# An LSTM step on one core: the low half of h in group 1 made in two operations, each with a wait of its own

## The chip, the cores and the metric

The kernel runs on 1 core of one Trainium2 chip. The metric is the device time of one execution in microseconds (us). TensorE multiplies matrices, VectorE (DVE in the rows), ScalarE (ACT) and GpSimd (POOL) work element by element, and SyncE (SP) issues transfers. The engines run side by side and wait for each other on semaphores. PE and PEld in the rows are TensorE's matmuls and its loads of the stationary operand.

## The reference

An LSTM over 512 steps, batch 16, 512 features, with a residual; one weight matrix for the input and one for h, all in fp32:

```python
xW = jnp.einsum('ntd,dg->ntg', x, Wx) + b
def step(carry, xw_t):
    prev_h, prev_c = carry
    a = xw_t + prev_h @ Wh
    i, f, o = (jax.nn.sigmoid(a[:, k * 512:(k + 1) * 512]) for k in range(3))
    g = jnp.tanh(a[:, 3 * 512:])
    next_c = f * prev_c + i * g
    next_h = o * jnp.tanh(next_c)
    return (next_h, next_c), next_h
x = x + jnp.swapaxes(hs, 0, 1)
```

(The gates are written shorter here than in the original; `hs` are the h of all steps.)

## The kernel before

**Numbers.** Each fp32 operand is split into an fp16 high part and an fp16 low part (what the high part leaves), so that a product is high times high, low times high and high times low. The weights are split once at the start. x is split in chunks of 16 steps, and h in every step. `h_halves[par]` holds for each of the 4 blocks of features (128 features each, 16 columns of batch) three slots of 16 columns: zeros, the high half, the low half. Slots 0 and 1 together are the stationary operand of `recurrent_low` (times the low weights), slots 1 and 2 that of `recurrent_high` (times the high weights).

**Groups.** The features of h come in two groups, `n` = 0 with blocks 0 and 1 and `n` = 1 with blocks 2 and 3. The gates' sums of a group lie in `acc[par][:, n]`, and each sum needs all four blocks of the h of the step before. A block takes four matmuls, one for each quarter of 32 rows of the array.

**TensorE in a step** (from L356): low weights with blocks 0 and 1 for both groups, when the high half of group 0 is there; high weights with blocks 0 and 1 for group 0, when the low half of group 0 is there; low weights with blocks 2 and 3 for group 0; then L363 waits for the low half of group 1, high weights with blocks 2 and 3 for group 0, and `acc_ready` goes up for the first time. The rest of group 1 follows, and `acc_ready` goes up again. Then come matmuls for the input of a later pair of steps (`input_part`, L303). L311 is the matmul of `recurrent_low`, L317 that of `recurrent_high`.

**VectorE in a step**, written out in order by hand: transpose group 0's sums when `acc_ready` allows it (`turn(0)`, L510), add the two halves (L514), transpose group 1's (L510), products of the gates (L523), L514 and new cell (L528) and so on. The end of the step, which the change touches, is: high half of h of group 0 (L538), new cell of group 1 (L528), `full_h(0)` (L542), `keep_cell(0)` (L532), `low_of_h(0)` (L547), `high_of_h(1)` (L538), `full_h(1)` (L542), `keep_cell(1)` (L532), `low_of_h(1)` (L547), and the output of the step (L575). L547 waits for L542. L538 waits for ScalarE's tanh of the cell (L270) and GpSimd's output gate (L194). L575 waits for the kept cell, L532.

**Behind the output** stands some work of preparing x, set by the place `at` of the step in its chunk: in steps 1 to 4 a quarter of the next chunk is searched for its largest value (L586), in 5 to 10 there are one or two operations of one to four columns (L590, L433, L436, L439, L443, L447, L450), in 12 to 15 the low half of a quarter of x is made (`low_of_x`, L493), and in 0 and 11 there is nothing. Chunk 0 also makes the last two quarters of its own x in its steps 1 and 2. The last chunk prepares nothing. Then the next step's `turn(0)` comes.

ScalarE does the tanh of the gates (L260, L265) and of the cell, opens the sums (L234, L237) and makes the high half of x (L216). GpSimd adds the output gate of group 0 (L186) and scales it (L194).

Of the kernel before, what the change touches and what calls it, by code (L numbers as in the profile page):

```python
# [5 lines left out]
ALU = mybir.AluOpType  # L6
# [9 lines left out]
NG = 2  # L16
# [7 lines left out]
def lstm_kernel(nc, x, h0, wx, wh, bias, out):  # L24
# [7 lines left out]
    with ExitStack() as ctx:  # L32
# [6 lines left out]
        def sem(name):  # L39
            return ctx.enter_context(nc.semaphore(name))  # L40
# [85 lines left out]
        acc_ready = sem("acc_ready")  # L126
# [10 lines left out]
        h_feat_ready = sem("h_feat_ready")  # L137
        h_ready = sem("h_ready")
# [150 lines left out]
        @block.tensor  # L289
        def _(pe):  # L290
            pe.wait_ge(ones_ready, 2)
            pe.wait_ge(tops_ready, 1)
            pe.matmul(wx_sums[:, 0:1], ones[:], tops[:, 0:1], start=True, stop=True).then_inc(sums_ready, 1)
            pe.wait_ge(x_top_ready, 1)
            pe.matmul(x_sums, ones_16[:], x_top[:], start=True, stop=True).then_inc(x_sum_ready, 1)
            pe.wait_ge(tops_ready, 2)
            pe.matmul(wh_sums[:, 1:3], ones[:], tops[:, 1:3], start=True, stop=True).then_inc(sums_ready, 1)

            def input_part(pair, of):
                for c in of:  # L300
                    for half, w in ((0, w_high["wx"]), (1, w_high["wx"]), (0, w_low["wx"])):
                        for j in range(Q):
                            last = pe.matmul(x_acc[pair % 2][32 * j:32 * j + 32], x_halves[:, pair % (CHUNK // 2), c, half],  # L303
                                             w[:, c].rearrange("p (n q) g -> p q n g", q=Q)[:, j],
                                             start=False, stop=False, skip_group_check=True)
                return last

            def recurrent_low(par, n, of):
                for c in of:
                    for j in range(Q):  # L310
                        pe.matmul(acc[par][32 * j:32 * j + 32, n, 0:GL], h_halves[1 - par][:, c, 0:2], w_low["wh"][:, c, n * Q + j],  # L311
                                  start=False, stop=False, skip_group_check=True)

            def recurrent_high(par, n, of):
                for c in of:
                    for j in range(Q):
                        last = pe.matmul(acc[par][32 * j:32 * j + 32, n, 0:GL], h_halves[1 - par][:, c, 1:3], w_high["wh"][:, c, n * Q + j],  # L317
                                         start=False, stop=c == C - 1, skip_group_check=True)
                return last

            pe.wait_ge(wx_low_done, C)
            pe.wait_ge(zeroed, 6)
            for p in range(2):
                for n in range(NG):
                    for j in range(Q):
                        opened = pe.matmul(acc[p][32 * j:32 * j + 32, n, 0:GL], h_halves[0][:, 0, 0:2], w_high["wx"][:, 0, j],
                                           start=True, stop=False, skip_group_check=True)
                    opened.then_inc(acc_opened, 1)
            for i in range(2):
                for j in range(Q):  # L330
                    opened = pe.matmul(x_acc[i][32 * j:32 * j + 32], h_halves[0][:, 0, 0:2],
                                       w_high["wx"][:, 0].rearrange("p (n q) g -> p q n g", q=Q)[:, j],
                                       start=True, stop=False, skip_group_check=True)
                opened.then_inc(acc_opened, 1)
            pe.wait_ge(x_ready, 1)
            pe.wait_ge(bias_placed, 1)
            input_part(0, (0, 1, 2, 3)).then_inc(x_summed, 1)
            pe.wait_ge(bias_placed, 2)
            input_part(1, (0, 1))
            pe.wait_ge(acc_filled, 1)  # L340
            pe.wait_ge(h_ready, NG)
            for c in range(C):
                pe.wait_ge(wh_low_done, c + 1)
                recurrent_low(0, 0, (c,))
                first = recurrent_high(0, 0, (c,))
                recurrent_low(0, 1, (c,))
                second = recurrent_high(0, 1, (c,))
                if c == C - 1:
                    first.then_inc(acc_ready, 1)
                    second.then_inc(acc_ready, 1)  # L350

            for t in range(T):
                par = t % 2
                chunk, at = divmod(t, CHUNK)
                if t > 0:
                    pe.wait_ge(h_high_ready, NG * t + 1)  # L356
                    recurrent_low(par, 0, (0, 1))
                    recurrent_low(par, 1, (0, 1))
                    pe.wait_ge(h_ready, NG * t + 1)
                    recurrent_high(par, 0, (0, 1))  # L360
                    pe.wait_ge(h_high_ready, NG * t + 2)
                    recurrent_low(par, 0, (2, 3))
                    pe.wait_ge(h_ready, NG * t + 2)  # L363
                    recurrent_high(par, 0, (2, 3)).then_inc(acc_ready, 1)
                    recurrent_high(par, 1, (0, 1))
                    recurrent_low(par, 1, (2, 3))
                    recurrent_high(par, 1, (2, 3)).then_inc(acc_ready, 1)
                if at == 6 and chunk + 1 < CHUNKS:
                    pe.wait_ge(x_top_ready, chunk + 2)
                    pe.matmul(x_sums, ones_16[:], x_top[:], start=True, stop=True).then_inc(x_sum_ready, 1)  # L370
                if t + 1 < T:
                    pair = (t + 3) // 2
                    if 2 * pair >= T:
                        pe.wait_ge(acc_filled, t + 2)
                    elif t % 2 == 1:
                        if at == 13:
                            pe.wait_ge(x_ready, QUARTERS * (chunk + 1) + 1)
                        pe.wait_ge(bias_placed, pair + 1)
                        input_part(pair, (0,))
                        pe.wait_ge(acc_filled, t + 2)  # L380
                        input_part(pair, (1,))
                    else:
                        input_part(pair, (2,))
                        pe.wait_ge(acc_filled, t + 2)
                        input_part(pair, (3,)).then_inc(x_summed, 1)

        @block.vector
        def _(dve):
# [60 lines left out]
            def inverses_of(par):  # L449
# [32 lines left out]
            dve.tensor_scalar(h_halves[1][:, :, 1, :], h0_feat[:], scales[0][:, 2:3], None, ALU.mult).then_inc(h_high_ready, NG)  # L482
            dve.wait_ge(h_high_ready, NG)
            dve.scalar_tensor_tensor(h_halves[1][:, :, 2, :], h0_feat[:], scales[0][:, 2:3], h_halves[1][:, :, 1, :],
                                     ALU.mult, ALU.subtract).then_inc(h_ready, NG)
            dve.wait_ge(b_loaded, 16)
            dve.tensor_scalar(b_rows[:, :, 64:GL], b_rows[:, :, 64:GL], 0.5, None, ALU.mult).then_inc(b_ready, 1)

# [12 lines left out]
            for t in range(T):  # L501
                par = t % 2
# [3 lines left out]
                nth = [NG * t + n + 1 for n in range(NG)]  # L506
# [24 lines left out]
                def keep_cell(n):  # L531
                    dve.scalar_tensor_tensor(gates[1 - par][n][:, 0, :], products[n][:, 0, :], 0.5, products[n][:, 1, :],  # L532
                                             ALU.mult, ALU.add).then_inc(cell_kept, 1)

                def high_of_h(n):
                    og, ct = (k.rearrange("p (c b) -> p c b", b=B) for k in (o_gate[n][:], cell_tanh[n]))
                    dve.wait_ge(h_parts_ready[n], 2 * (t + 1))
                    dve.tensor_tensor(h_halves[par][:, 2 * n:2 * n + 2, 1, :], og, ct, ALU.mult).then_inc(h_high_ready, 1)  # L538
# [2 lines left out]
                    og, ct = (k.rearrange("p (c b) -> p c b", b=B) for k in (o_gate[n][:], cell_tanh[n]))  # L541
                    dve.tensor_tensor(h_feat[par][:, 2 * n:2 * n + 2, :], og, ct, ALU.mult).then_inc(h_feat_ready, 1)  # L542

                def low_of_h(n):
                    cs = slice(2 * n, 2 * n + 2)
                    dve.wait_ge(h_feat_ready, nth[n])
                    dve.tensor_tensor(h_halves[par][:, cs, 2, :], h_feat[par][:, cs, :], h_halves[par][:, cs, 1, :], ALU.subtract)\  # L547
                        .then_inc(h_ready, 1)

# [11 lines left out]
                new_cell(1)  # L561
                full_h(0)
                keep_cell(0)
                low_of_h(0)
                high_of_h(1)
                full_h(1)
                keep_cell(1)
                low_of_h(1)
                dve.wait_ge(cell_kept, NG * (t + 1))

                half, slot = divmod(at, HALF)
# [76 lines left out]
```

## Time and profile before

| | |
|---|---|
| median of 3 runs | 1855.11 us (1855.08 to 1855.83) |
| the profiled execution, its own time | 1856.47 us |
| its span in the profile | 1854.4 us |
| busy: VectorE, TensorE matmuls, TensorE loads, ScalarE, GpSimd | 92%, 90%, 57%, 55%, 29% |
| instructions of VectorE | 9739 |

The span is that of the instructions in the trace; the device time includes some 2 us around it. Busy time adds the recorded durations. On VectorE and TensorE one instruction often begins before the recorded end of the one in front, so a gap smaller than that overlap shows as no idle time; starts are read from the rows in order of time.

### The profile page before, as it was taken

The page shows a single profiled execution, that of the slowest core. Times are in us where ns is not written, and L with a number is a line of the kernel's source. Part 1 is how long each engine was busy: PE and PEld are TensorE (multiplying, and loading weights), DVE is VectorE, ACT ScalarE, POOL GpSimd, SP SyncE. Part 2 cuts the span into 40 slices and gives each one's busy share as a digit, 9 for nine tenths or more (in the row PEclk, how much of TensorE's full clock was granted, in tenths as well). Part 3 has the DMA queues.
Part 4 walks back from the last instruction along what each step waited for, and adds up shares of the span by engine and source line. Part 5 has one row for each costly group of instructions (what it writes and reads, how often), then busy time and mean ns, then how long its engine had stood idle before and what let it go on. Part 6 is the DMA issues. An engine that isn't in the chain of part 4 may idle for free.

```text
span 1854.4 us, 106048 instructions
## 1 busy us (share of the span) xinstructions
PE 1674.3 (90%) x45116; PEld 1065.3 (57%) x45116; DVE 1713.2 (92%) x9739; ACT 1011.4 (55%) x3985; POOL 539.3 (29%) x1560
## 2 busy tenths in 40 slices
PE   1999999999999999999999999999999999999997
PEld 0555555555555555555555555555555555555555
DVE  8999999999999999999999999999999999999998
ACT  4555555555555555555555555555555555555554
POOL 0222223322332222233223332222232233322222
PEclk9999999999999999999999999999999999999999
DMA  5000000000000000000000000000000000000000
GB/s 210 15 26 21 21 23 23 21 21 26 21 21 26 21 21 21 26 21 21 26 21 21 26 21 21 21 27 21 21 26 21 21 24 24 21 21 27 18 12 14
DMA packets 39067, 49.03 MB, mean 26 GB/s; under 512 B 4416, under 2 KB 36160, under 8 KB 38592
## 3 DMA queue, kind: packets, MB, share of 16 engines
q1 hardware_dynamic: 37152, 37.77, 6.3%
q8 instruction: 352, 5.77, 1.3%
q10 hardware_dynamic: 1440, 4.49, 0.6%
q14 instruction: 123, 1.01, 0.2%
HBM read 25.46 MB, written 16.78 MB: 23 GB/s over the span
## 4 chain that ended last, share of the span: by engine, by line
DVE 70%; PE 19%; ACT 7%; issue 3%; DMA 1%; ACTq 0%; DVEq 0%
DVE turned L510 22%; DVE mailbox L514 13%; PE acc L311 12%; DVE products L523 11%; ACT gates L260 7%; PE acc L317 7%; DVE h_halves L538 5%; DVE h_halves L547 3%; DVE gates L532 3%; DVE x_halves L493 3%; DVE out_ring L575 3%; DVE h_feat L542 3%; DVE x_tops L586 2%; DVE mailbox L528 2%; DMA wh<-in_wh 1%
## 5 line engine op out<-in xcount | busy, mean ns | idle before, releaser
L311 PE MATMUL acc<-wh_low,h_halves 128*32 128x256 f16 x16384 | 719.4, 274 | 135.6 <-DVE h_halves L538 133.8
L317 PE MATMUL acc<-wh_high,h_halves 128*32 128x256 f16 x16384 | 722.3, 275 | 0.0
L303 PE MATMUL x_acc<-wx_high,x_halves 128*32 128x512 f16 x8192 | 621.5, 380 | 1.1 <-ACT x_acc L234 1.1
L311 PEld LDWEIGHTS acc<-wh_low,h_halves 128*32 128x32 f16 x16384 | 390.5, 96 | 395.3 <-DVE h_halves L538 383.8
L260 ACT ACTIVATE gates<-mailbox 128x96 f32<-128x96 f32 x1024 | 257.1, 251 | 634.1 <-DVE mailbox L514 634.1
L510 DVE STREAM_TRANSPOSE turned<-acc 128x256 f32<-128x256 f32 x1024 | 458.9, 448 | 57.2 <-PE acc L317 51.4
L194 POOL TENSOR_SCALAR o_gate<-gates,scales 128x32 f32<-128x32 f32 x1024 | 372.7, 364 | 419.4 <-ACT gates L265 419.4
L186 POOL TENSOR_TENSOR o_preact<-turned 128x32 f32<-128x32 f32 x512 | 163.4, 319 | 892.0 <-DVE turned L510 892.0
L317 PEld LDWEIGHTS acc<-wh_high,h_halves 128*32 128x32 f16 x16384 | 343.6, 96 | 113.8
L303 PE MATMUL x_acc<-wx_low,x_halves 128*32 128x512 f16 x4096 | 399.2, 380 | 0.0
L237 ACT ACTIVATE acc<-x_acc,step_mask 128x512 f32<-128x512 f32 x512 | 334.8, 654 | 4.7 <-PE x_acc L303 4.7
L514 DVE TENSOR_TENSOR mailbox<-turned 128x96 f32<-128x96 f32 x1024 | 270.2, 264 | 17.6
L303 PEld LDWEIGHTS x_acc<-wx_high,x_halves 128*32 128x32 f16 x8192 | 216.7, 97 | 117.3 <-issue 3.7
L523 DVE SCALAR_TENSOR_TENSOR products<-gates 128x64 f32<-128x64 f32 x1024 | 230.4, 225 | 55.3
L270 ACT ACTIVATE mailbox<-mailbox 128x32 f32<-128x32 f32 x1024 | 191.5, 187 | 163.7 <-DVE mailbox L528 163.7
L265 ACT ACTIVATE gates<-o_preact 128x32 f32<-128x32 f32 x1024 | 231.9, 226 | 0.0
L528 DVE SCALAR_TENSOR_TENSOR mailbox<-products 128x32 f32<-128x32 f32 x1024 | 200.9, 196 | 0.0
L547 DVE TENSOR_TENSOR h_halves<-h_feat,h_halves 128x32 f16<-128x32 f32 x1024 | 196.6, 192 | 0.0
L538 DVE TENSOR_TENSOR h_halves<-o_gate,mailbox 128x32 f16<-128x32 f32 x1024 | 189.5, 185 | 0.0
L532 DVE SCALAR_TENSOR_TENSOR gates<-products 128x32 f32<-128x32 f32 x1024 | 189.5, 185 | 0.0
L542 DVE TENSOR_TENSOR h_feat<-o_gate,mailbox 128x32 f32<-128x32 f32 x1024 | 184.1, 180 | 0.0
L303 PEld LDWEIGHTS x_acc<-wx_low,x_halves 128*32 128x32 f16 x4096 | 109.9, 97 | 112.0 <-issue 1.0
(67 smaller groups left out, 696.5 us busy)
## 6 DMA issues: line engine op xcount, KB each, us to landing
out<-out_ring SPq DMA_DIRECT2D x128, 128.0 KB, 2.1
x_ring<-in_x SPq DMA_DIRECT2D x120, 128.0 KB, 2.9
wx<-in_wx ACTq DMA_DIRECT2D x4, 512.0 KB, 8.1
wx<-in_wx SPq DMA_DIRECT2D x4, 512.0 KB, 8.1
wh<-in_wh SPq DMA_DIRECT2D x4, 512.0 KB, 16.7
wh<-in_wh ACTq DMA_DIRECT2D x4, 512.0 KB, 17.1
x_ring<-in_x SPq DMA_DIRECT2D x2, 512.0 KB, 16.7
b_rows<-in_b ACTq DMA_DIRECT2D x1, 256.0 KB, 21.4
```

The source lines that it names most:

```text
L194: pool.tensor_scalar(o_gate[n][:], gates[par][n][:, 4, :], 1.0, scales[following][:, 1:2], ALU.add, ALU.mult)\
L237: act.activation(acc[t % 2][:, :, 0:GL], x_acc[t // 2 % 2][:], ACT.Copy, scale=step_mask[:, t % 2:t % 2 + 1])\
L260: act.activation(gates[par][n][:, 1:4, :], preact[n].rearrange("p (g c) b -> p g (c b)", c=2), ACT.Tanh, scale=rescale[chunk % 2]).then_in ...
L303: last = pe.matmul(x_acc[pair % 2][32 * j:32 * j + 32], x_halves[:, pair % (CHUNK // 2), c, half], w[:, c].rearrange("p (n q) g -> p q n g ...
L311: pe.matmul(acc[par][32 * j:32 * j + 32, n, 0:GL], h_halves[1 - par][:, c, 0:2], w_low["wh"][:, c, n * Q + j], start=False, stop=False, sk ...
L317: last = pe.matmul(acc[par][32 * j:32 * j + 32, n, 0:GL], h_halves[1 - par][:, c, 1:3], w_high["wh"][:, c, n * Q + j], start=False, stop=c ...
L510: dve.transpose(turned[n][:].rearrange("p g s b -> p (g s b)"), acc[par][:, n, 0:GL]).then_inc(turned_ready, 1)
L514: dve.tensor_tensor(preact[n], turned[n][:, 0:6, 0, :], turned[n][:, 0:6, 1, :], ALU.add)\
L523: dve.scalar_tensor_tensor(products[n][:], gates[par][n][:, 2:4, :], 1.0, gates[par][n][:, 0:2, :], ALU.add, ALU.mult).then_inc(products_r ...
L532: dve.scalar_tensor_tensor(gates[1 - par][n][:, 0, :], products[n][:, 0, :], 0.5, products[n][:, 1, :], ALU.mult, ALU.add).then_inc(cell_k ...
L538: dve.tensor_tensor(h_halves[par][:, 2 * n:2 * n + 2, 1, :], og, ct, ALU.mult).then_inc(h_high_ready, 1)
L547: dve.tensor_tensor(h_halves[par][:, cs, 2, :], h_feat[par][:, cs, :], h_halves[par][:, cs, 1, :], ALU.subtract)\
```

## The change

`low_of_h` took a group and made the low half of both of its blocks in one operation. It now takes the first block, the number of blocks and the number of the `full_h` of this step that it waits for. Group 0 is made in one operation as before. Group 1 is made in two operations in a row, block 2 and block 3, each of which counts up `h_ready`. TensorE waits for the first ahead of the high weights with block 2, and for the second ahead of those with block 3. `h_ready` goes up three times a step instead of two, and its waits are counted so.

```diff
-            pe.wait_ge(h_ready, NG)
+            pe.wait_ge(h_ready, 3)
...
-                    pe.wait_ge(h_ready, NG * t + 1)
+                    pe.wait_ge(h_ready, 3 * t + 1)
                     recurrent_high(par, 0, (0, 1))
                     pe.wait_ge(h_high_ready, NG * t + 2)
                     recurrent_low(par, 0, (2, 3))
-                    pe.wait_ge(h_ready, NG * t + 2)
-                    recurrent_high(par, 0, (2, 3)).then_inc(acc_ready, 1)
+                    pe.wait_ge(h_ready, 3 * t + 2)
+                    recurrent_high(par, 0, (2,))
+                    pe.wait_ge(h_ready, 3 * t + 3)
+                    recurrent_high(par, 0, (3,)).then_inc(acc_ready, 1)
...
-                                     ALU.mult, ALU.subtract).then_inc(h_ready, NG)
+                                     ALU.mult, ALU.subtract).then_inc(h_ready, 3)
...
-                def low_of_h(n):
-                    cs = slice(2 * n, 2 * n + 2)
-                    dve.wait_ge(h_feat_ready, nth[n])
+                def low_of_h(first, blocks, kept):
+                    cs = slice(first, first + blocks)
+                    dve.wait_ge(h_feat_ready, NG * t + kept)
...
-                low_of_h(0)
+                low_of_h(0, 2, 1)
                 high_of_h(1)
                 full_h(1)
                 keep_cell(1)
-                low_of_h(1)
+                low_of_h(2, 1, 2)
+                low_of_h(3, 1, 2)
                 dve.wait_ge(cell_kept, NG * (t + 1))
```

## Rows read from the trace of the kernel before

**Rows 1.** The page: busy time, the clock by slices, the chain that ended last

```profile
PE 1674.3 (90%) x45116; PEld 1065.3 (57%) x45116; DVE 1713.2 (92%) x9739; ACT 1011.4 (55%) x3985; POOL 539.3 (29%) x1560
...
PEclk9999999999999999999999999999999999999999
...
DVE 70%; PE 19%; ACT 7%; issue 3%; DMA 1%; ACTq 0%; DVEq 0%
```

**Rows 2.** The waits: who waited for whom, us in total, times, longest

```profile
PE acc L311 <- DVE h_halves L538: 133.8, 480, 1.7
DVE turned L510 <- PE acc L317: 51.4, 201, 0.4
```

**Rows 3.** Timeline of VectorE (start us, us, ...): first and last opening transpose

```profile
51.18 0.45 DVE L510 STREAM_TRANSPOSE turned<-acc 128x256 f32<-128x256 f32 x1
...
1848.96 0.45 DVE L510 STREAM_TRANSPOSE turned<-acc 128x256 f32<-128x256 f32 x1 [0.38 <-PE acc L317]
```

**Rows 4.** Timeline of all engines, end of a step with nothing behind L575

```profile
1010.95 0.18 DVE L542 TENSOR_TENSOR h_feat<-o_gate,mailbox 128x32 f32<-128x32 f32 x1
...
1011.05 0.19 DVE L532 SCALAR_TENSOR_TENSOR gates<-products 128x32 f32<-128x32 f32 x1
...
1011.16 0.19 DVE L547 TENSOR_TENSOR h_halves<-h_feat,h_halves 128x32 f16<-128x32 f32 x1
1011.20 0.39 PE L311 MATMUL acc<-wh_low,h_halves 128*32 128x256 f16 x8
...
1011.27 0.28 DVE L575 SCALAR_TENSOR_TENSOR out_ring<-h_feat,inverses,x_ring 128x64 f32<-128x64 f32 x1
1011.41 0.34 PEld L317 LDWEIGHTS acc<-wh_high,h_halves 128*32 128x32 f16 x16
...
1011.86 0.45 DVE L510 STREAM_TRANSPOSE turned<-acc 128x256 f32<-128x256 f32 x1 [0.31 <-PE acc L317]
```

**Rows 5.** Timeline of VectorE: ends of steps with L493, and with L586

```profile
1007.75 0.28 DVE L575 SCALAR_TENSOR_TENSOR out_ring<-h_feat,inverses,x_ring 128x64 f32<-128x64 f32 x1
1007.95 0.48 DVE L493 SCALAR_TENSOR_TENSOR x_halves<-x_ring,scales,x_halves 128x256 f16<-128x256 f32 x1
1008.35 0.45 DVE L510 STREAM_TRANSPOSE turned<-acc 128x256 f32<-128x256 f32 x1
...
1014.79 0.28 DVE L575 SCALAR_TENSOR_TENSOR out_ring<-h_feat,inverses,x_ring 128x64 f32<-128x64 f32 x1
1014.99 0.41 DVE L586 TENSOR_REDUCE x_tops<-x_ring 128x1 f32<-128x256 f32 x1
1015.38 0.45 DVE L510 STREAM_TRANSPOSE turned<-acc 128x256 f32<-128x256 f32 x1
```

**Rows 6.** Timeline of VectorE in chunk 0: L493 and L586 in one step

```profile
57.81 0.48 DVE L493 SCALAR_TENSOR_TENSOR x_halves<-x_ring,scales,x_halves 128x256 f16<-128x256 f32 x1
58.21 0.41 DVE L586 TENSOR_REDUCE x_tops<-x_ring 128x1 f32<-128x256 f32 x1
58.54 0.44 DVE L510 STREAM_TRANSPOSE turned<-acc 128x256 f32<-128x256 f32 x1
```

**Rows 7.** Groups of instructions: form xcount | busy us, mean ns | idle before

```profile
L547 DVE TENSOR_TENSOR h_halves<-h_feat,h_halves 128x32 f16<-128x32 f32 x1024 | 196.6, 192 | 0.0
...
L532 DVE SCALAR_TENSOR_TENSOR gates<-products 128x32 f32<-128x32 f32 x1024 | 189.5, 185 | 0.0
...
L443 DVE TENSOR_SCALAR acc_scale<-x_scale_bits,scale_bits,top_scale 128x1 f32<-128x1 f32 x32 | 8.6, 270 | 0.1
```

**Rows 8.** Timeline of VectorE before the steps: operations of one column in a row

```profile
33.81 0.14 DVE L466 COPY factors<-inverse_bits 128x1 f32<-128x1 f32 x1
33.87 0.14 DVE L467 TENSOR_SCALAR factors<-inverse_bits 128x1 f32<-128x1 f32 x1
```

**Rows 9.** L317 (1011.38 to 1011.6) and L311 (one step): ns min/median/max

```profile
L317 PE MATMUL acc<-wh_high,h_halves x8: 272/275/278, 1011.4 to 1011.5; 128*32 128x256 f16 x8
...
L311 PE MATMUL acc<-wh_low,h_halves x32: 272/273/283, 1010.5 to 1012.0; 128*32 128x256 f16 x32
```

## The prediction

> **What bounds the kernel now.** I read the page first. VectorE is busy 92% of the span, TensorE 90% at the full clock (the granted clock is 9 or more tenths in every slice, which is the 2.4 GHz level), and the chain that ended last runs 70% through VectorE and 19% through TensorE [rows 1]. So the kernel is one chain of 512 steps, and the waits say where it changes hands: TensorE waits for the high half of h (L538) in 480 cases, VectorE waits for TensorE's sum before the transpose (L510) in 201 cases, and nobody is listed as waiting for the low half (L547) [rows 2]. First and last opening transpose are 1797.78 us apart, 511 steps of 3.518 us on the mean [rows 3].
>
> Then I read one step in order of time, because a list of idle time hides ties. In a plain step (1011 us) the second L547 starts at 1011.16, L575 at 1011.27, and the next transpose only at 1011.86 after 0.31 us of idling for TensorE [rows 4]. So here TensorE sets the end: its loads of the stationary operand for `recurrent_high(par, 0, (2, 3))` start at 1011.41, and 0.45 us later the transpose starts. In a step that also makes the low half of x (L493), the order is L575 at 1007.75, L493 at 1007.95, transpose at 1008.35, and in one that searches x (L586) L575 at 1014.79, L586 at 1014.99, transpose at 1015.38 [rows 5]. All three kinds of step take the same 3.52 us from transpose to transpose (1008.35, 1011.86, 1015.38 [rows 4, 5]). The question is whether VectorE has slack in the last two. The first chunk tells: there L493 and L586 stand one behind the other, with no wait between them: L493 at 57.81, L586 at 58.21, transpose at 58.54, and TensorE is long done [rows 6]. L493 therefore holds VectorE for 0.40 us and L586 for 0.33 us by themselves. L575 plus L493 is 0.20 + 0.40 = 0.60 us from L575 to the transpose, against 0.59 us (1011.27 to 1011.86) that TensorE needs anyway. **In steps with L493 VectorE has no slack at all; with L586 it has 0.59 - 0.20 - 0.33 = 0.06 to 0.07 us; in all others at least 0.2 us** (the largest of the small operations behind L575 takes 0.27 us, L443 [rows 7], and VectorE operations free their engine about 0.08 us before their recorded end: L542 takes 0.18 and the next starts 0.10 behind it [rows 4]).
>
> **The change, part by part.**
> 1. VectorE: one 128x32 operation at the end of the step becomes two of 128x16, so 512 more operations. L547 takes 192 ns, L532 of the same width 185 ns [rows 7]. By width, L586 (256 columns, 0.41 us) against L532 (32) is 1.0 ns a column and L493 (256, 0.48 us) 1.3 ns [rows 5, 7]; so 16 columns less save 16 to 21 ns: I take 17, or 175 ns an operation (an estimate). What counts for the queue is start to start. L542 takes 0.18 us and the next operation starts 0.10 us behind it [rows 4]; I take the overlap as 83 ns, so that L547 holds VectorE for 192 - 83 = 109 ns, which agrees with the 0.11 us from L547 to L575. A piece: 175 - 83 = 92; I take 91 ns, so the two hold VectorE for 0.182 instead of 0.109 us: **+73 ns** for L575 and all behind it. Bounds: an operation of one element holds it about 62 ns (0.06 from 33.81 to 33.87 [rows 8]), +15 ns; a piece as dear as a whole operation, 109 ns, +109 ns. 91 is the value of the slope between these ends, the upper one being the nearer row (the same operation). The wait of the second piece on `h_feat_ready` is met already by the first, so it costs nothing.
> 2. TensorE: the wait is split. Block 2's low half ends at 1011.16 + 0.175 = 1011.335, 17 ns earlier than now, and with the 0.05 us from the end of L547 to the load (1011.35 to 1011.41 [rows 4]) its loads could start at 1011.39. But the matmuls before them (8 of L311 from 1011.20, two batches of four side by side at 0.11 us a batch) hold the array until 1011.41, so only the lateness of the load goes. That lateness is visible: the first matmuls behind this wait took 278 ns, the ordinary ones 272 to 273 [rows 9]. Gain: **-6 ns** at most on TensorE's path, bounds 0 and -6.
> 3. Block 3's low half starts one piece later, 1011.25, and ends at 1011.43; its loads can start at 1011.48. Its matmuls are due one batch behind those of block 2, at 1011.41 + 0.11 = 1011.52, and a load that comes just in time costs 10 ns (283 against 273 ns for L311 behind its wait [rows 9]). So it is ready with 0.03 us to spare and the second wait costs nothing. If that cover is gone (a piece over 0.12 us start to start), each ns comes onto every step. Queued behind it on TensorE are the last four matmuls of group 0, whose end the transpose waits for, and all of group 1.
> 4. The counts `3 * t + ...` of `h_ready`, the initial increment by 3, and the call for group 0 change no instruction.
>
> Where the stall goes: in a plain step TensorE is still last, 6 ns earlier. In a step with L493 the transpose starts 73 ns later, since VectorE had no slack. In one with L586, 73 less the slack of 66 is +7 ns. The chain from a transpose on is unchanged, the second transpose of a step follows its own predecessor (L514), so the late transposes move everything behind them.
>
> Sum over 511 intervals, taken from the profiled execution:
> - 31 chunks x 4 steps with L493 = 124, x 73 ns = +9.05 us
> - 124 steps with L586 x 7 ns = +0.87 us; two of them, in chunk 0, have L493 as well and pay 66 more: +0.13 us
> - the other 263 x -6 ns = -1.58 us
> In all **+8.5 us**. The profiled execution was 1856.47 us (span 1854.4), 1.36 above the median of the runs, 1855.11. On the median: 1855.11 + 8.5 = **1863.6 us**, +0.46%.
>
> The Trainium skill ("VectorE: DVE Perf Modes", the TRN2 errata) states a fixed cost for each SBUF operation, 58 cycles plus one per column at 0.96 GHz, and warns that many small tiles pay it each time. By that an operation of 32 columns is 94 ns (the 0.10 us between L542 and L532 agrees) and one of 16 is 77 ns; the shift would be +60 ns and the sum, an estimate with that page's figures, +5.2 us, so 1860.3.
>
> **The rivals.**
> - *Pieces nearly as dear as the whole* (as forecast, larger term). For it: L532 and L547 differ in what they write and read, not in width, by 7 ns, and by the slopes above the whole width of 32 is 32 to 42 of the 192 ns. At 109 ns a piece: 124 x 109 + 124 x 43 = +18.9 us, no gain on TensorE (block 3 becomes ready at 1011.51, just in time): 1874.0. Between this and the forecast all is possible; 1 in 10 for the upper half of it.
> - *Not slower: the added operation is hidden and only TensorE's gain is left.* Place: the interval L493 to transpose. If L493 frees VectorE 0.07 us sooner than its 0.40 us, the transposes wait for TensorE in all steps, and 511 x -6 ns = -3.1 us: 1852.0. It decides when the pair costs no more than the old one, that is under 0.055 us a piece, or when L493 has slack. For it: 0.395 is just what TensorE's time leaves, and such a tie looks like a wait for TensorE. Against it: the same 0.40 us stands at 57.81, where the next operation waits for nobody. 7 in 100.
> - *A piece waits until the one in front has ended*, the pieces in series at 0.175 us. L575 would start 0.158 us later: 124 x 158 = +19.6, 124 x 92 = +11.4 us; block 3 would be ready at 1011.56 and its matmuls at 1011.57 instead of 1011.52, some +49 ns in the other 263: +12.9. Sum +43.9 us: 1899.0. Against it: L532 starts well before the end of L542 [rows 4]. 3 in 100. The Trainium skill ("VectorE: DVE Perf Modes", "The DRAIN you can't avoid") says that the next operation does not start until the pipe is empty; the rows here show starts some 80 ns ahead of the recorded end, so the trace does not bear out that rule in this form.
> - *TensorE pays for the second wait.* Place: the load for block 3, which can no longer run a whole batch ahead. Its price is 10 ns where it is late: 263 x (10 + 6) = +4.2 us on the sum above, 1867.8. From 0.12 us a piece on. 8 in 100, inside my range.
>
> **How the numbers follow.** Forecast, the term between +50 and +95 ns: 72 in 100, 1859 to 1870. Dearer pieces 10, second wait 8, serial 3, hidden 7. No change that can be measured here is within 0.2%, 3.7 us (1851.4 to 1858.8). Hidden falls within it, with -0.17%, and so do very cheap pieces. Slower by more 0.88, same 0.09, faster 0.03. At +50 ns a step the sum is 6.2 - 0.7 - 1.6 = +3.9 us, 1859.0; the range goes to 1858 below, and above to 1873, near the sum of the bound of 109 ns.
>
> **What would show each step.** Two operations of 128x16 at about 175 ns, 90 ns apart; L575 0.18 instead of 0.11 us behind the first; steps with L493 at 3.59 us, those with L586 at 3.52, plain ones at 3.511; 0.20 + 0.40 us from L575 to transpose in the first; the first matmuls of block 2 at 273 instead of 278 ns; no idle time of TensorE in front of block 3. The prediction is wrong if steps with L493 keep 3.517 us, if plain steps lengthen, or if a piece takes over 0.2 us.

## The result: 1861.4 us, 0.33% slower

The changed kernel takes 1861.41 us (median of 7 runs, 1861.28 to 1861.64); the kernel before took 1855.23 us beside it (7 runs, 1855.08 to 1855.83). That is +6.2 us, a ratio of 1.0033 with a 95% interval of 1.0021 to 1.0045. The interval goes from +3.9 to +8.3 us. The forecast was 1863.6 us, +8.5, just above it.

The profiled execution after took 1861.64 us, its span is 1859.5 us. Page of the kernel after: busy time, then the chain that ended last by engine.

```profile
PE 1672.8 (90%) x45116; PEld 1071.7 (58%) x45116; DVE 1737.4 (93%) x10251; ACT 1012.0 (54%) x3985; POOL 540.4 (29%) x1560
...
DVE 71%; PE 17%; ACT 8%; issue 3%; DMA 1%; ACTq 0%; DVEq 0%
```

VectorE has 512 instructions and 24 us more; the chain has moved from TensorE to VectorE, as far as a share of 2 points shows it. The waits say the same: the transpose waits visibly for TensorE in 171 steps, where it was 201 [rows 2].

```profile
DVE turned L512 <- PE acc L317: 34.1, 171, 0.4
```

Groups by form after the change (mean ns behind the comma). `low_of_h` is now L549, the transpose L512, the output L578, the low half of x L495, the search of x L589.

```profile
L549 DVE TENSOR_TENSOR h_halves<-h_feat,h_halves 128x16 f16<-128x16 f32 x1024 | 133.8, 172 | 0.0
L549 DVE TENSOR_TENSOR h_halves<-h_feat,h_halves 128x32 f16<-128x32 f32 x512 | 98.2, 192 | 0.0
```

A piece takes 172 ns on the mean (175 was estimated), 175 the first and 169 the second: half the width saves 20 of 192 ns. Now the end of a step of each kind, in order of time. First a plain step (place 11), the counterpart of [rows 4].

```profile
996.56 0.26 DVE L549 TENSOR_TENSOR h_halves<-h_feat,h_halves 128x16 f16<-128x16 f32 x2
996.59 0.39 PE L311 MATMUL acc<-wh_low,h_halves 128*32 128x256 f16 x8
996.74 0.28 DVE L578 SCALAR_TENSOR_TENSOR out_ring<-h_feat,inverses,x_ring 128x64 f32<-128x64 f32 x1
996.79 0.35 PEld L317 LDWEIGHTS acc<-wh_high,h_halves 128*32 128x32 f16 x16
996.81 0.61 PE L317 MATMUL acc<-wh_high,h_halves 128*32 128x256 f16 x16
...
997.25 0.45 DVE L512 STREAM_TRANSPOSE turned<-acc 128x256 f32<-128x256 f32 x1 [0.23 <-PE acc L317]
```

The output starts 0.18 us behind the first piece, not 0.11. TensorE's loads start at 996.79, 0.02 us ahead of the matmuls. Before, in the step of [rows 4], loads and matmuls both read 1011.41:

```profile
1011.41 0.62 PE L317 MATMUL acc<-wh_high,h_halves 128*32 128x256 f16 x16
```

There is no idle time in front of the matmuls with block 3: by the starts in the two traces they come 109 ns behind those with block 2 on the mean over all steps, where it was 115 ns before. The first eight of these matmuls (four with block 2, four with block 3), by duration (min/median/max):

```profile
L317 PE MATMUL acc<-wh_high,h_halves x8: 272/273/273, 996.8 to 996.9; 128*32 128x256 f16 x8
```

The 278 ns of [rows 9] are gone. Then steps with L495 (1004.40 to 1007.98 to 1011.55) and with L589, the counterparts of [rows 5]:

```profile
1004.40 0.45 DVE L512 STREAM_TRANSPOSE turned<-acc 128x256 f32<-128x256 f32 x1
...
1007.21 0.26 DVE L549 TENSOR_TENSOR h_halves<-h_feat,h_halves 128x16 f16<-128x16 f32 x2
1007.38 0.28 DVE L578 SCALAR_TENSOR_TENSOR out_ring<-h_feat,inverses,x_ring 128x64 f32<-128x64 f32 x1
1007.58 0.48 DVE L495 SCALAR_TENSOR_TENSOR x_halves<-x_ring,scales,x_halves 128x256 f16<-128x256 f32 x1
1007.98 0.44 DVE L512 STREAM_TRANSPOSE turned<-acc 128x256 f32<-128x256 f32 x1
...
1011.55 0.44 DVE L512 STREAM_TRANSPOSE turned<-acc 128x256 f32<-128x256 f32 x1
...
1015.04 0.45 DVE L512 STREAM_TRANSPOSE turned<-acc 128x256 f32<-128x256 f32 x1 [0.23 <-PE acc L317]
...
1025.06 0.28 DVE L578 SCALAR_TENSOR_TENSOR out_ring<-h_feat,inverses,x_ring 128x64 f32<-128x64 f32 x1
1025.25 0.41 DVE L589 TENSOR_REDUCE x_tops<-x_ring 128x1 f32<-128x256 f32 x1
1025.58 0.44 DVE L512 STREAM_TRANSPOSE turned<-acc 128x256 f32<-128x256 f32 x1
```

From output to transpose it is still 0.20 + 0.40 us with L495: no slack, as read in [rows 5, 6]. These steps take 3.58 and 3.57 us. With L589 it is 0.19 + 0.33 us, so VectorE sets the end there too now, by a few ns. And the step behind the last late one, 1011.55 to 1015.04, takes 3.49 us by these starts (3496 ns), less than the shortest step of before (3503 ns). That was not foreseen. A transpose is called late here when VectorE comes free only after TensorE's sum is there; note that the late transposes read 0.44 and those that wait for TensorE 0.45.

The intervals between opening transposes, averaged by place over the chunks (without the first and the last) from their starts in the two traces, are this (after minus before, ns): places 12 to 15 **+66, +59, +59, +60**; place 1 +2, places 2 to 4 -8, -7, -9; places 0 and 5 **-16, -17**; the other six -4 to -9, -7 on the mean. The two steps of chunk 0 that have L495 and L589 behind each other are 68 and 56 ns longer. All 511 together are 1854.07 - 51.62 = 1802.45 us against 1797.78 us [rows 3], +4.7 us:

```profile
51.62 0.45 DVE L512 STREAM_TRANSPOSE turned<-acc 128x256 f32<-128x256 f32 x1 [0.38 <-PE acc L317]
...
1854.07 0.45 DVE L512 STREAM_TRANSPOSE turned<-acc 128x256 f32<-128x256 f32 x1 [0.31 <-PE acc L317]
```

The two profiled executions differ by 5.2 us, the medians by 6.2.

### The profile page after: what moved, and what is told of

The parts are those of the page before. It is cut to its first block, busy times and chain, and to the rows that moved or that the text cites. A ratio compares the mean times of both kernels' runs of the same rounds, so it can differ in the third digit from the quotient of the medians.

```text
span 1859.5 us, 106560 instructions
## 1 busy us (share of the span) xinstructions
PE 1672.8 (90%) x45116; PEld 1071.7 (58%) x45116; DVE 1737.4 (93%) x10251; ACT 1012.0 (54%) x3985; POOL 540.4 (29%) x1560
## 4 chain that ended last, share of the span: by engine, by line
DVE 71%; PE 17%; ACT 8%; issue 3%; DMA 1%; ACTq 0%; DVEq 0%
DVE turned L512 21%; DVE mailbox L516 13%; DVE products L525 11%; PE acc L311 10%; ACT gates L260 7%; PE acc L317 6%; DVE h_halves L549 5%; DVE h_halves L540 5%; DVE gates L534 3%; DVE out_ring L578 3%; DVE h_feat L544 3%; DVE x_halves L495 3%; DVE x_tops L589 2%; DVE mailbox L530 2%; DMA wh<-in_wh 1%
## 5 line engine op out<-in xcount | busy, mean ns | idle before, releaser
L311 PE MATMUL acc<-wh_low,h_halves 128*32 128x256 f16 x16384 | 719.3, 274 | 141.9 <-DVE h_halves L540 140.4
L317 PE MATMUL acc<-wh_high,h_halves 128*32 128x256 f16 x16384 | 719.3, 274 | 0.0
L311 PEld LDWEIGHTS acc<-wh_low,h_halves 128*32 128x32 f16 x16384 | 390.5, 96 | 401.2 <-DVE h_halves L540 390.3
L512 DVE STREAM_TRANSPOSE turned<-acc 128x256 f32<-128x256 f32 x1024 | 455.8, 445 | 38.6 <-PE acc L317 34.1
L317 PEld LDWEIGHTS acc<-wh_high,h_halves 128*32 128x32 f16 x16384 | 349.7, 95 | 106.0
L549 DVE TENSOR_TENSOR h_halves<-h_feat,h_halves 128x16 f16<-128x16 f32 (+1 forms) x1536 | 232.1, 178 | 0.0
```

Source lines behind the costliest of these rows:

```text
L512: dve.transpose(turned[n][:].rearrange("p g s b -> p (g s b)"), acc[par][:, n, 0:GL]).then_inc(turned_ready, 1)
```

## The experiments

Each run was timed beside runs of the kernel before on the same chip; that kernel's time differs a little between chips (1853.7 to 1856.5 us), so differences and ratios are given, not bare times.

**1. The pieces without the split wait (e1_wait_both).** What is TensorE's part of the change, the split wait, worth?

```diff
-                    pe.wait_ge(h_ready, 3 * t + 2)
-                    recurrent_high(par, 0, (2,))
                     pe.wait_ge(h_ready, 3 * t + 3)
+                    recurrent_high(par, 0, (2,))
                     recurrent_high(par, 0, (3,)).then_inc(acc_ready, 1)
```

> The change with its two pieces, but TensorE waits for both in front of block 2. Theory (the sum of the prediction): the pieces hold VectorE 0.093 and 0.085 us and the second ends 0.262 us behind the start of the first, where the one operation ended after 0.192. TensorE's loads start 0.070 us later than before in every step, so all 511 intervals grow by about 70 ns: 1855.2 + 35.8 = 1891 us, and steps with L493 are no longer than the others. Rival: TensorE's own queue hides the late half and only VectorE's tail matters: as the change, 1861.4.

Measured 1888.69 against 1853.72 us, +35.0 us, ratio 1.0189 (1.0173 to 1.0204). The timeline of this kernel, loads of TensorE for block 2 and the next transpose in a step with the low half of x:

```profile
1024.85 0.26 DVE L548 TENSOR_TENSOR h_halves<-h_feat,h_halves 128x16 f16<-128x16 f32 x2
...
1025.16 0.34 PEld L317 LDWEIGHTS acc<-wh_high,h_halves 128*32 128x32 f16 x16 [0.17 <-DVE h_halves L548]
...
1025.62 0.45 DVE L511 STREAM_TRANSPOSE turned<-acc 128x256 f32<-128x256 f32 x1
```

The loads stand idle for 0.17 us for the second piece and start 0.31 us behind the first. All steps take about 3.58 us, whatever stands behind the output, 64 to 71 ns more at every place than in e5_spread_before (below), whose trace is from the same chip. So the matmuls with block 2 do sit on the path, and the split wait hides the second piece entirely. It undoes a loss that the pieces themselves make.

**2. A second wait and nothing else (e2_wait_twice).**

```diff
-                    recurrent_high(par, 0, (2, 3)).then_inc(acc_ready, 1)
+                    recurrent_high(par, 0, (2,))
+                    pe.wait_ge(h_ready, NG * t + 2)
+                    recurrent_high(par, 0, (3,)).then_inc(acc_ready, 1)
```

> The kernel before, one operation for group 1, but a second wait on the same value between block 2 and block 3. Theory: a wait that is already met costs TensorE nothing: the time of before, plain steps unchanged. Rival: the second wait costs about 10 ns on each step, +5 us, and would explain most of the change by itself.

Measured 1856.40 against 1856.49 us, ratio 0.9999 (0.9990 to 1.0008). A wait that was met long before costs TensorE nothing that can be measured. This run alone does not cover the changed kernel, where the second piece comes only shortly before it is needed; there the 109 ns from block 2 to block 3 and the 273 ns of their matmuls, shown above, say the same. The rival falls.

**3. One more operation of 16 columns, for nobody (e3_extra_piece).**

```diff
                 low_of_h(1)
+                dve.tensor_tensor(spare[par][:, 3:4, 2, :], h_feat[par][:, 3:4, :], h_halves[par][:, 3:4, 1, :], ALU.subtract)\
+                    .then_inc(spare_done, 1)
```

(The spare tile and its semaphore are declared besides.)

> The kernel before plus one operation of 16 columns into a spare tile behind the low half of group 1 in each step (work added, nothing waits for it). Theory: VectorE's tail grows by 85 ns, TensorE's path stays. 124 steps with L493 x 85 = +10.5 us, 124 with L586 x (85 - 66) = +2.4 us, others 0; a step that begins with a transpose held up by VectorE alone is 8 ns shorter (as in the changed kernel), 248 x -8 = -2.0 us. Sum +10.9: 1866.1 us. Without that give-back 1868.1. Rival, the tail hides the operation: 1855.2 us.

Measured 1865.33 against 1853.72 us, +11.6 us, ratio 1.0062 (1.0047 to 1.0078). End of a step with L495 in this kernel:

```profile
1009.16 0.19 DVE L549 TENSOR_TENSOR h_halves<-h_feat,h_halves 128x32 f16<-128x32 f32 x1
1009.27 0.17 DVE L571 TENSOR_TENSOR spare<-h_feat,h_halves 128x16 f16<-128x16 f32 x1
1009.35 0.28 DVE L579 SCALAR_TENSOR_TENSOR out_ring<-h_feat,inverses,x_ring 128x64 f32<-128x64 f32 x1
1009.55 0.48 DVE L495 SCALAR_TENSOR_TENSOR x_halves<-x_ring,scales,x_halves 128x256 f16<-128x256 f32 x1
1009.95 0.44 DVE L512 STREAM_TRANSPOSE turned<-acc 128x256 f32<-128x256 f32 x1
```

The operation holds VectorE for 0.08 us, and it is paid in the steps with work on x alone: VectorE's tail by itself makes a loss of the size forecast, with TensorE's part untouched. L549 holds VectorE for 0.11 us here too, with an operation behind it that waits for nothing. So the 0.11 us from L547 to L575 in [rows 4], where L575 also waits for L532, are the time that L547 holds the engine.

The give-back is what a late transpose seems to return to the next interval. The total lies between the sums with and without it (10.9 and 12.9), so it does not decide on that. The rows point to it: against e5_spread_before on the same chip, place 12 has +88 ns and places 13 to 15 have +77 to +79, and places 0 and 5, which follow the last late transposes, have -9 and -12. The next two runs were made for it.

**4. Transposes made late on purpose (e6_late_10, e7_late_150).**

```diff
+                if at in (0, 11):
+                    dve.tensor_reduce(spare[:, at % 2:at % 2 + 1], b_rows[:].rearrange("p n g -> p (n g)")[:, 0:330], AX.X, ALU.max)\
+                        .then_inc(spare_done, 1)
```

(e7_late_150 has 460 columns instead of 330. The spare tile and its semaphore are declared besides.)

> The kernel before plus a maximum over 330 columns of a constant tile into a spare column (work added) behind the output at places 0 and 11 of each chunk but the last, where nothing stood. By the rows of L586 (256 columns hold VectorE 0.33 us) it holds it about 0.405 us, 10 ns more than TensorE needs. Theory (give-back): the transpose there starts about 10 ns later, takes 441 instead of 449 ns, and the next interval is 8 ns shorter, so that the sum is within 0.5 us of before. Rival: a late transpose costs its whole lateness, 62 x 10 ns = +0.6 us, and its duration stays at 449 ns.

> As e6_late_10 with 460 columns, some 145 ns later than TensorE's sum. Theory: the give-back is a fixed 8 ns for a transpose that has nothing to wait for, not a share of the lateness: 62 x (145 - 8) = +8.5 us over before. Rival: more time comes back with more lateness, since TensorE is further ahead in the next step: under +7 us.

Measured: with 330 columns 1857.12 against 1856.49 us, ratio 1.0003 (0.9994 to 1.0012); with 460 columns 1865.50, +9.0 us, ratio 1.0049 (1.0033 to 1.0064). Neither total can tell the theories apart (+0.6 with an interval of -1.1 to +2.2 us, and +9.0 with one of +6.1 to +11.9); the rows can. Timeline of e6_late_10: the transposes before, at and after the late one.

```profile
1008.71 0.45 DVE L512 STREAM_TRANSPOSE turned<-acc 128x256 f32<-128x256 f32 x1
...
1011.82 0.49 DVE L585 TENSOR_REDUCE spare<-b_rows 128x1 f32<-128x330 f32 x1
1012.23 0.44 DVE L512 STREAM_TRANSPOSE turned<-acc 128x256 f32<-128x256 f32 x1
...
1015.73 0.45 DVE L512 STREAM_TRANSPOSE turned<-acc 128x256 f32<-128x256 f32 x1
```

The same late transpose, and the one of the next step, which waited for TensorE (ns min/median/max, of one):

```profile
L512 DVE STREAM_TRANSPOSE turned<-acc x1: 437/437/437, 1012.2 to 1012.2; 128x256 f32<-128x256 f32 x1
...
L512 DVE STREAM_TRANSPOSE turned<-acc x1: 449/449/449, 1015.7 to 1015.7; 128x256 f32<-128x256 f32 x1
```

The late one is shorter, and the interval behind it is 3.50 us where 3.52 is usual. Averaged over the chunks (without the first and the last), from the transposes' starts: the interval at place 11 is 3526 ns and the next one 3507, against 3516 elsewhere: +10, then -9. At place 0 it is 3530 and 3507. With 460 columns it is 3663 and 3509 at place 11, against 3517: +146, then -8; at place 0 it is 3669 and 3509. Timeline of e7_late_150:

```profile
1013.45 0.45 DVE L512 STREAM_TRANSPOSE turned<-acc 128x256 f32<-128x256 f32 x1
...
1017.11 0.44 DVE L512 STREAM_TRANSPOSE turned<-acc 128x256 f32<-128x256 f32 x1
...
1020.62 0.45 DVE L512 STREAM_TRANSPOSE turned<-acc 128x256 f32<-128x256 f32 x1
```

So what comes back is some 8 ns for each late transpose, not a share of the lateness. Why a late transpose is shorter is not shown.

**5. The work on x spread out (e4_spread_after, e5_spread_before).** If the loss sits in the steps with L493 alone, then cutting L493 in halves and putting them where VectorE has slack must turn the change into a gain, and must do nothing for the kernel before.

```diff
-            def low_of_x(chunk, q):
-                two = slice(QUARTER // 2 * q, QUARTER // 2 * (q + 1))
+            def low_of_x(chunk, first, pairs=1):
+                two = slice(first, first + pairs)
...
+                if chunk > 0 and at in (0, 5, 6, 10):
+                    low_of_x(chunk, {0: 4, 5: 5, 6: 6, 10: 7}[at])
```

(The calls at places 12 to 15 stay, now with one pair each; TensorE's wait at place 13 is counted in pairs, and one at place 11 is added for the last pair.)

> The change, with the low half of x made in single pairs of steps (128 columns, 0.26 us) at the places 12, 13, 14, 15, 0, 5, 6, 10 instead of 256 columns at 12 to 15, so that no step has 0.40 us behind the output. Theory: the loss of the change sits in the L493 steps alone and TensorE's gain of some 8 ns a step stays: 1855.2 - 511 x 0.008 = 1851 us. Rival: the added operation costs in all steps, the time stays near 1861.

> The kernel before with the low half of x spread in the same way. Theory: all steps wait for TensorE already, nothing is won: 1855 us (within 1.5). Rival: steps with L493 were bound by VectorE by more than the tie shows, then it is faster by over 2 us.

Measured: the change with spread work 1850.22 us, 3.5 us below the kernel before, ratio 0.9981 (0.9972 to 0.9990). The kernel before with spread work 1854.09 against 1853.72 us, ratio 1.0004 (0.9995 to 1.0013). The gain over the kernel before is under 0.2%, but its interval does not reach 1. Timeline of e4_spread_after, a step with a half L493 (L497 there) at its end, from its opening transpose to the next:

```profile
991.40 0.45 DVE L514 STREAM_TRANSPOSE turned<-acc 128x256 f32<-128x256 f32 x1 [0.24 <-PE acc L317]
...
994.39 0.28 DVE L580 SCALAR_TENSOR_TENSOR out_ring<-h_feat,inverses,x_ring 128x64 f32<-128x64 f32 x1
994.59 0.34 DVE L497 SCALAR_TENSOR_TENSOR x_halves<-x_ring,scales,x_halves 128x128 f16<-128x128 f32 x1
994.91 0.45 DVE L514 STREAM_TRANSPOSE turned<-acc 128x256 f32<-128x256 f32 x1
```

This is the version that beats both kernels. By the starts of transposes, its steps at places 12 to 15 take 3505 ns, those of e5_spread_before 3510 to 3511, in profiles taken on one chip: by them TensorE's gain from the split wait is 5 to 6 ns a step. The medians of the two kernels differ by more, 3.9 us or 7.6 ns a step, and the profiled execution of e4_spread_after was 1.1 us above the median of its runs, 2 ns a step if all of that lies in the steps. So the gain lies somewhere between 5 and 8 ns; the 8 ns of the expectation are at its upper end.

## Why the prediction was right, and its sizes

Point by point, in its own terms.

- *VectorE's term, +73 ns in 124 steps.* Right in place and mechanism. The pieces hold VectorE for 93 and 85 ns (from the starts in the trace; 91 and 91 were taken) instead of 109: +69 ns. e3_extra_piece shows the same kind of loss by VectorE alone.
- *L493 has no slack, L586 66 ns.* Right: the transposes behind L495 start 0.40 us after it as before, and those behind L589 have become bound by VectorE. e4 and e5 show it from the other side: without 0.40 us behind the output the loss is gone, and the kernel before wins nothing by it, so its transposes there were just in balance with TensorE. Place 12 grew by 66 of the 69 ns, so the slack with L493 was some 3 ns and not quite none. The two steps of chunk 0 paid 68 and 56 ns, as foreseen.
- *TensorE's gain, -6 ns a plain step, second wait free.* Right: 278 became 273 ns, block 3 follows block 2 after 109 instead of 115 ns, e2 gives zero for the wait, e4 against e5 gives 5 to 8 ns. In the first pair of profiles the six plain places that follow no late transpose have -7. The profiled execution before was 1.2 us above the median of its runs and the one after 0.2 us; if that difference lies in the steps, it is 2 ns a step, and the -7 would be -5.
- *The step that was mis-sized* is "The chain from a transpose on is unchanged". The prediction let nothing come back from a late transpose. One that is late because VectorE was busy is some 8 ns shorter than one released by TensorE at that moment (442 to 443 against 450 to 451), and the chain behind it starts 7 to 10 ns earlier. There are 248 late transposes, behind the 124 steps with L495 and the 124 with L589, and each shortens the next interval: that is why places 13 to 15 have +59 and place 12 has +66, and why 0 and 5, which follow the last late ones, have -16 and -17.

The sum with measured sizes: 124 x 66 = +8.2, 124 x 2 = +0.2, the two steps of chunk 0 +0.1 more, 263 x -7 = -1.8, 248 x -8 = -2.0, together +4.7 us, as in the trace. These sizes are read from the same intervals, so the agreement says only that no step is left over; their causes are what the runs show. Of the 3.8 us between this and the +8.5 of the forecast, the late transposes gave back 2.0; the steps with L493 cost 66 instead of 73 ns (0.9 us) and those with L586 2 instead of 7 ns (0.6 us). Shown by runs of their own are the first (e3, e4), the absence of a wait's cost (e2) and the give-back (e6, e7). The medians differ by 6.2 us, 1.5 more than the steps in the two profiles. Of this 0.4 us lies ahead of the first transpose (51.62 against 51.18 us), and the profiled execution before was 1.2 us above the median of its runs, the one after 0.2. In which part of the execution that last 1.0 us lies is open, since only one execution of each has a trace.

Of the rivals, "pieces nearly as dear as the whole" is out by 93 and 85 ns a piece where the whole has 109. "Pieces in series" is out by the 0.09 us between the pieces: here VectorE starts the second operation some 80 ns before the recorded end of the first. The prediction quotes one half of the section of the Trainium skill ("VectorE: DVE Perf Modes", "The DRAIN you can't avoid"), that the next operation waits for an empty pipe; the same section adds that a next operation that is not held starts earlier. Such an earlier start is what the trace shows here. "TensorE pays for the second wait" is out by e2 and by the 109 ns from block 2 to block 3. "Hidden" was what the change would have been without the tie: with the work on x spread it comes true, with -3.5 us where it was priced at -3.1. The estimates from the formula of the Trainium skill ("VectorE: DVE Perf Modes", the TRN2 errata), 94 ns for 32 columns and 77 ns for 16, were both low: L547 holds VectorE for 109 ns and a piece for 85 to 93. That the sum by them, 1860.3 us, came nearer to 1861.4 than the forecast is luck: the shift of 60 ns was too small (69 measured), which made up for the give-back that it lacked as well.

## What to carry to other kernels

Before an operation is cut in two to release a waiting engine sooner, add the cost of the second piece at the end of that queue and look for the steps in which that queue has nothing to spare; a mean slack over the steps says nothing about the quarter of them that have none. Two engines can be tied to within a few nanoseconds (3 here) while the profile shows no wait at the tie: start times against the length of time that each operation holds its engine, taken where nothing else interferes, show it. If such a tie is the obstacle, moving the tied work into steps with slack can make the cut worth its price.

## What the runs showed of the hardware that had not been expected

The same 128x256 transpose of a PSUM tile took 448 to 451 ns when its semaphore came last and 436 to 443 ns when its engine came free last (medians by place over the kernels), and what follows it starts 8 to 12 ns earlier. TensorE shows the like: the matmuls behind a load that waited for its semaphore take 278 ns (L317) or 283 ns (L311) instead of 272 to 273 [rows 9]. In both cases the recorded start seems to hold some of the time that the release takes; that is a reading, and no run here separates it. Half the width of a 128x32 operation saved 20 of its 192 ns, and the second of the two pieces held the engine for 85 ns, the first for 93, with the same shape; why, no run shows.
